# Attention scores from two rounded products of relu(m) and a linear part gathered with each source's row

## The reference, cut to what matters

```python
xl = (x @ Wl).reshape(n, H, D)
xr = (x @ Wr).reshape(n, H, D)
msg = xl[src] + xr[dst]
act = jnp.where(msg > 0, msg, NEG_SLOPE * msg)
e = jnp.einsum('ehd,hd->eh', act, att)
m = jax.ops.segment_max(e, dst, num_segments=n)
p = jnp.exp(e - m[dst])
denom = jax.ops.segment_sum(p, dst, num_segments=n)
alpha = p / (denom[dst] + 1e-16)
out = jax.ops.segment_sum(alpha[..., None] * xl[src], dst, num_segments=n)
```

## Time and profile before

| | |
|---|---|
| median of 3 runs | 1490.02 (1489.29 to 1491.17) |
| the profiled execution, its own time | 1491.28 |
| its span in the trace | 1489.5 |
| TensorE (PE) busy, share of the span | 1410.9, 95% |
| VectorE (DVE) | 781.9, 52% |
| ScalarE (ACT) | 424.5, 29% |
| GpSimd (POOL) | 255.5, 17% |
| the chain that ended last | PE 57%, DVE 1%; its lines L1946 35%, L1967 18% are the dense layers |

### The profile page before, as it was taken

The page is one execution under the profiler, slowest core; times in us unless marked ns, Lnnn a source line. Parts: engine busy times, 40 slices in busy tenths (PEclk is TensorE's granted clock), DMA queues, the critical chain, the costliest instruction groups (busy, mean ns, idle before and its releaser), DMA issues.

```text
span 1489.5 us, 17808 instructions
## 1 busy us (share of the span) xinstructions
PE 1410.9 (95%) x6845; PEld 1144.6 (77%) x6845; DVE 781.9 (52%) x1359; ACT 424.5 (29%) x716; POOL 255.5 (17%) x307
## 2 busy tenths in 40 slices
PE   3888999959999999899999999999999999999997
PEld 3886888836666666678888888888888888888886
DVE  6996777538888888645346621410133332410244
ACT  7862323246666664212111100201200000210000
POOL 3000000057777673100000000000010100000000
PEclk9997999979999999999999999999999999999999
DMA  1666344456556652432127443230066544400253
GB/s 48 188 181 207 107 106 140 96 161 212 167 167 172 208 170 70 144 121 95 54 92 248 157 182 116 90 114 0 1 217 221 183 130 142 159 1 0 78 191 128
DMA packets 102404, 195.97 MB, mean 132 GB/s; under 512 B 27143, under 2 KB 61752, under 8 KB 102320
## 3 DMA queue, kind: packets, MB, share of 16 engines
q1 hardware_dynamic: 77866, 121.28, 27.2%
q0 software_dynamic: 22640, 73.09, 14.2%
q10 hardware_dynamic: 1814, 0.47, 0.2%
HBM read 140.87 MB, written 53.92 MB: 131 GB/s over the span
## 4 chain that ended last, share of the span: by engine, by line
PE 57%; DVE 1%; DMA 0%; DVEq 0%; issue 0%; ACT 0%; POOL 0%
PE layers_y_ps L1946 35%; PE layers_y_ps L1967 18%; PE layers_turn_ps L1930 2%; PE layers_up_ps L1913 1%; PE layers_y_ps L1983 1%; DMA x_d<-fetched_x 0%; DVE layers_w_lo L2102 0%; DVE layers_y L2146 0%; PE layers_y_ps L1991 0%; DVE layers_y L605 0%; DVE layers_ln_stats L599 0%; PE layers_turn_ps L1901 0%; DVE layers_parts_lo L2119 0%; DVEq L600 0%; PE layers_y_ps L1901 0%
## 5 line engine op out<-in xcount | busy, mean ns | idle before, releaser
L517 POOL DMA_INDIRECT attention_got<-xl_d,heads_first_src x156 | 162.1, 1039 | 61.6 <-issue 43.8
L1967 PE MATMUL layers_y_ps<-layers_parts_hi,layers_counts 128*128 128x512 f32 x464 | 143.0, 389 | 0.0
L1967 PE MATMUL layers_y_ps<-layers_parts_lo,layers_counts 128*128 128x512 f32 x464 | 142.9, 389 | 0.0
L1946 PE MATMUL layers_y_ps<-layers_w_hi,layers_parts_hi 128*128 128x512 f32 x400 | 125.4, 395 | 0.0
L1946 PE MATMUL layers_y_ps<-layers_w_lo,layers_parts_hi 128*128 128x512 f32 x400 | 123.3, 389 | 0.0
L1946 PE MATMUL layers_y_ps<-layers_w_hi,layers_parts_lo 128*128 128x512 f32 x400 | 123.2, 389 | 0.0
L1967 PEld LDWEIGHTS layers_y_ps<-layers_parts_lo,layers_counts 128*128 128x128 f32 x464 | 87.1, 188 | 18.1
L1967 PEld LDWEIGHTS layers_y_ps<-layers_parts_hi,layers_counts 128*128 128x128 f32 x464 | 86.9, 188 | 17.9
L2119 DVE SCALAR_TENSOR_TENSOR layers_parts_lo<-layers_y_ps,layers_parts_hi 128x1024 fp32r<-128x1024 f32 x16 | 19.6, 1225 | 144.7 <-ACT layers_parts_hi L2062 144.7
L1334 PE MATMUL attention_row_ps<-attention_bent,edges_att_rows 128*128 128x512 f32 x184 | 95.4, 601 | 0.0
L1367 PE MATMUL attention_mix_ps<-attention_weighted,attention_hot 128*110 128x260 f32 x368 | 95.1, 382 | 0.0
(11 more groups left out here) (338 smaller groups left out, 2792.1 us busy)
## 6 DMA issues: line engine op xcount, KB each, us to landing
layers_counts<-counts_d SPq DMA_DIRECT2D x30, 640.0 KB, 4.0
layers_rest<-x_d SPq DMA_DIRECT2D x23, 512.0 KB, 3.9
self_d<-layers_y POOLq DMA_DIRECT2D x20, 512.0 KB, 5.6
x_d<-layers_y POOLq DMA_DIRECT2D x19, 512.0 KB, 2.9
fetched_x<-x_d SPq DMA_DIRECT2D x17, 512.0 KB, 3.6
fetched_raw<-in_L_gnn_W_self POOLq DMA_DIRECT2D x16, 512.0 KB, 5.7
fetched_raw<-in_L_gnn_W_neigh POOLq DMA_DIRECT2D x16, 512.0 KB, 8.9
heads_dst_wide<-in_dst_held SPq DMA_DIRECT2D x13, 512.0 KB, 4.6
```

The lines of the kernel that those rows point to most:

```text
L517: nc.gpsimd.indirect_dma_start(got[:, t, :], None, xl_d, bass.IndirectOffsetOnAxis(src[:, a * QUAD + t:a * QUAD + t + 1], 0))\
L1946: last = nc.tensor.matmul(y_ps[n % 2][:, a:a + HALF], rows_in[t][:, k * P:(k + 1) * P], w[k][:, a:a + HALF], start=(k == 0 and p == 0), st ...
L1967: last = nc.tensor.matmul(y_ps[n % 2][:, a:a + HALF], counts[c % 2][:, k, :], part[k][:, a:a + HALF], start=(k == 0 and part is hi), stop= ...
```

## The change

It uses act = 0.2 m + 0.8 relu(m). The linear part 0.2 m . att is 0.2 xl . att of the source plus 0.2 xr . att of the target. The target's is the same for all edges of a target and leaves the softmax as it is, so it is left out. The source's is computed once per node in the front, stored in 16 more columns of the node's row in xl_d (of which 4 are used, a row is now 1088 B) and so gathered with it; ScalarE copies it out of `got` (`take_linear`, twice a visit) and TensorE turns it as the first part of `row_ps` (`turn_linear`). For relu(m), ScalarE makes the rounded part (`bent_hi`) and VectorE the remainder (`bent_lo`), and the score is two f32r products in place of one float32 product. The attention vector is split in a rounded and a low part as well, placed in two sets of rows; `pick` sums the two sets in `spread`, and a 128x8 matrix `fold` sums them in `turn`, which is now a float32 product with 8 moving columns and no longer a transpose. The diff, cut to its core:

```diff
+XL_ROW = HID + LINE
...
+            nc.vector.tensor_scalar(g["folded_row"][:, :], row[:, :], float(QUADS * HEADS), -float(QUADS * HEADS),
+                                    ALU.is_ge, ALU.mult)
             dve.drain()
+            nc.vector.tensor_tensor(g["folded_row"][:, :], g["folded_row"][:, :], row[:, :], ALU.add)
...
             nc.vector.tensor_scalar(g["pick"][:, :, :],
                                     g["iota"][:, 0:QUADS * HEADS].unsqueeze(2).to_broadcast([P, QUADS * HEADS, PART]),
-                                    row[:, :], None, ALU.is_equal)
+                                    g["folded_row"][:, :], None, ALU.is_equal)
+            nc.vector.tensor_scalar(g["fold"][:, :], g["iota"][:, 0:QUADS * HEADS], g["folded_row"][:, :], None,
+                                    ALU.is_equal)
...
-        xl = m.sb("xl", [P, 2, HID])
+        xl = m.sb("xl", [P, 2, XL_ROW])
...
             def store_heads(tile):
                 u = tile % 2
-                sp.wait_ge(s["xl_ready"], tile + 1)
+                sp.wait_ge(s["linear_ready"], tile + 1)
                 sp.dma_start(rows(xl_d, tile), xl[:, u, :]).then_inc(xl_stored[u], 16)
...
                 dve.wait_ge(s["xl_ready"], tile + 1)
-                nc.vector.tensor_tensor(loop_sum[:, :], xr_ps[:, :], xl[:, u, :], ALU.add)\
+                linear = xl[:, u, HID:HID + HEADS]
+                nc.vector.scalar_tensor_tensor(out=linear_sum, in0=xl[:, u, 0:HID], scalar=SLOPE,
+                                               in1=att_row[:, :], op0=ALU.mult, op1=ALU.mult)
+                nc.vector.tensor_tensor(loop_sum[:, :], xr_ps[:, :], xl[:, u, 0:HID], ALU.add)\
                     .then_inc(s["xr_ready"], 1)
                 dve.drain()
-                nc.vector.scalar_tensor_tensor(out=loop_sum[:, :], in0=loop_sum[:, :], scalar=SLOPE,
-                                               in1=loop_sum[:, :], op0=ALU.mult, op1=ALU.max)
+                nc.vector.tensor_reduce(linear, linear_sum.rearrange("p (h d) -> p h d", h=HEADS), AX.X, ALU.add)\
+                    .then_inc(s["linear_ready"], 1)
+                nc.vector.tensor_scalar(loop_sum[:, :], loop_sum[:, :], 0.0, 1.0 - SLOPE, ALU.max, ALU.mult)
                 dve.drain()
...
-                                        AX.X, ALU.add).then_inc(s["xr_whole"], 1)
+                                        AX.X, ALU.add)
+                dve.drain()
+                scores = loop_score[:, u, :].rearrange("p (t k) -> p k t", t=2)
+                nc.vector.tensor_tensor(scores, scores, linear.rearrange("p (k t) -> p k t", t=2), ALU.add)\
+                    .then_inc(s["xr_whole"], 1)
...
-                    nc.vector.tensor_copy(g["att_rows"][r:r + PART, k, HEADS + h:HEADS + h + 1], att[r:r + PART, k:k + 1])
+                    nc.vector.tensor_scalar(g["att_rows"][r:r + PART, k, HEADS + h:HEADS + h + 1],
+                                            att[r:r + PART, k:k + 1], 1.0 - SLOPE, None, ALU.mult)
+                dve.drain()
+                for h in range(HEADS):
+                    k, r = h // 2, h % 2 * PART
+                    nc.vector.scalar_tensor_tensor(
+                        out=g["att_rows"][r:r + PART, k, 3 * HEADS + h:3 * HEADS + h + 1], in0=att[r:r + PART, k:k + 1],
+                        scalar=1.0 - SLOPE, in1=g["att_rows"][r:r + PART, k, HEADS + h:HEADS + h + 1].bitcast(F32),
+                        op0=ALU.mult, op1=ALU.subtract)
...
-        got = [first_got] + slots("got", [P, QUAD, HID], F32, GOT - 1)
+        got = [first_got] + slots("got", [P, QUAD, XL_ROW], F32, GOT - 1)
...
-        nothing = m.sb("nothing", [ROWS - SUB * SUBS, HEAD_DIM])
+        nothing = linear[0:ROWS - SUB * SUBS, 0, P - HEAD_DIM:]
...
+        def shifted_rows(j):
+            return far[j % 3][:, 0:HALF]
...
+            def turn_linear(j):
+                pe.wait_ge(linear_ready, QUADS * (j + 1))
+                for t in range(QUAD):
+                    nc.tensor.matmul(row_ps[j % 2][:, t * P:(t + 1) * P], linear[:, t, :], g["ident"][:, :],
+                                     is_transpose=True, start=(t == 0), stop=False, skip_group_check=True)
+
             def score(i):
                 j, a, k = i // UNITS, i % UNITS // KH, i % KH
                 pe.wait_ge(bent_ready, i + 1)
-                nc.tensor.matmul(row_ps[j % 2][:, :], g["att_rows"][:, k, (1 - a) * HEADS:(1 - a) * HEADS + P],
-                                 bent[i % 3][:, :], start=(i % UNITS == 0), stop=(i % UNITS == UNITS - 1),
-                                 skip_group_check=True).then_inc(scored, 1)
+                for part in (bent_hi, bent_lo):
+                    last = nc.tensor.matmul(row_ps[j % 2][:, :], g["att_rows"][:, k, (1 - a) * HEADS:(1 - a) * HEADS + P],
+                                            part[i % len(part)][:, :], start=False,
+                                            stop=(i % UNITS == UNITS - 1 and part is bent_lo), skip_group_check=True)
+                last.then_inc(scored, 1)
...
-                    last = nc.tensor.matmul(row_ps[j % 2][:, t * P:(t + 1) * P], shifted_rows[:, t * P:(t + 1) * P],
-                                            g["ident"][:, :], is_transpose=True, start=(t == 0),
+                    last = nc.tensor.matmul(row_ps[j % 2][:, t * P:t * P + QUADS * HEADS],
+                                            shifted_rows(j)[:, t * P:(t + 1) * P], g["fold"][:, :], start=(t == 0),
                                             stop=(t == QUAD - 1), skip_group_check=True)
...
+                if q == 2 and i < LAST:
+                    turn_linear(j)
                 if 2 <= i < LAST + 2:
                     score(i - 2)
...
-                nc.scalar.activation(scaled[i % 2][:, :], message_ps[i % 2][:, :], ACT.Copy, scale=SLOPE)\
-                    .then_inc(scaled_ready, 1)
+                nc.scalar.activation(bent_hi[i % 3][:, :], message_ps[i % 2][:, :], ACT.Relu).then_inc(high_ready, 1)
+
+            def take_linear(j, a):
+                act.wait_ge(*gathered(j, a))
+                nc.scalar.activation(linear[:, :, a * HEADS:(a + 1) * HEADS], held(j, a)[:, :, HID:HID + HEADS],
+                                     ACT.Copy).then_inc(linear_ready, 1)
...
                 if i < LAST:
                     scale(i)
+                if q == 0 and i < LAST:
+                    if j == 0:
+                        act.wait_ge(linear_cleared, 1)
+                    take_linear(j, 0)
...
                 if q == 1 and 1 <= j <= SUBS:
                     take_rows(j - 1)
+                if q == 1 and i < LAST:
+                    take_linear(j, 1)
...
             def bend(i):
-                dve.wait_ge(scaled_ready, i + 1)
-                nc.vector.tensor_tensor(bent[i % 3][:, :], message_ps[i % 2][:, :], scaled[i % 2][:, :], ALU.max)\
+                dve.wait_ge(high_ready, i + 1)
+                if i >= 2:
+                    dve.wait_ge(scored, i - 1)
+                nc.vector.scalar_tensor_tensor(out=bent_lo[i % 2][:, :], in0=message_ps[i % 2][:, :], scalar=0.0,
+                                               in1=bent_hi[i % 3][:, :].bitcast(F32), op0=ALU.max, op1=ALU.subtract)\
                     .then_inc(bent_ready, 1)
...
-                                        held(j, half)[:, :, :].rearrange("p t (h d) -> p (t h) d", h=HEADS),
+                                        held(j, half)[:, :, 0:HID].rearrange("p t (h d) -> p t h d", h=HEADS),
...
-            nc.vector.memset(nothing[:, :], 0.0).then_inc(nothing_made, 1)
+            nc.vector.memset(linear[:, :, :], 0.0).then_inc(linear_cleared, 1)
...
-    xl_d, mixed_d = dram("xl_d", [ROWS, HID]), dram("mixed_d", [ROWS, HID])
+    xl_d, mixed_d = dram("xl_d", [ROWS, XL_ROW]), dram("mixed_d", [ROWS, HID])
```

More of the change, by code:

```diff
@@ L636, in front_stage @@
         loop_sum = m.sb("loop_sum", [P, HID])
+        linear_sum = w.raw[:, KB - 1, :]
         loop_score = m.sb("loop_score", [P, 2, HEADS])
@@ L909, in take_heads @@
                     act.wait_ge(xl_stored[u], 16 * (tile // 2))
-                nc.scalar.activation(xl[:, u, :], xl_ps, ACT.Copy).then_inc(s["xl_ready"], 1)
+                nc.scalar.activation(xl[:, u, 0:HID], xl_ps, ACT.Copy).then_inc(s["xl_ready"], 1)
             split_x(0)
@@ L1066, in limit_edges @@
                 nc.vector.tensor_copy(g["rounds"][:, 1:2], rounds[:, :])
+            nc.vector.memset(xl[:, :, HID:], 0.0)
             split_x(0)
@@ L1266, in _ @@
             load(2)
[L1267 removed]
+            sp.wait_ge(linear_cleared, 1)
             for h in range(HEADS):
[L1269 removed]
+                sp.dma_start(mixed_d[SUB * SUBS:ROWS, h * HEAD_DIM:(h + 1) * HEAD_DIM], nothing)\
                     .then_inc(nothing_stored, 16)
@@ L1459, in take_shifted @@
                 act.wait_ge(shifted, j + 1)
-                nc.scalar.activation(shifted_rows[:, :], row_ps[j % 2][:, :], ACT.Copy).then_inc(shifted_out, 1)
```

(1 more changed line is left out.)

39 lines of the change are left out of this document (19 added, 20 removed).

## The result

The changed kernel took 1497.38 (median of 7 runs, 1494.16 to 1499.55) beside 1489.29 of the kernel before (7 runs, 1488.87 to 1491.17): ratio 1.0049, interval 1.0037 to 1.006. Its profiled execution took 1497.38 with a span of 1495.6, 6.1 above the span of before. It is slower by 8, inside the range, by more than the +1.4 of the sum.

What follows compares the result with a forecast made beforehand. DVE's chain, not PE, was taken to pace attention's visits. Terms 0.15 + 2.75 - 0.5 - 2.8 + 0.8 + 1.0 = +1.4 gave a median of 1491.4; range 1488.5 to 1498.8.

Steps and rivals of the forecast that it cites:

- the 0.67: Attention: DVE's wait per visit for the spread product, a DVE-PE-DVE round trip that stays; 13.4 to 14 in 20 visits.
- the -2.8 for arrears: Attention, visits 3 to 22: shorter scores save only the 2.8 us that a PE queue in arrears cost DVE.
- The clamp's slip: Attention: the longer turn delays the clamp by 0.08 in the ten visits without a weight half on DVE, +0.8 together.
- more than two: Attention, a sign of the forecast: DVE waits for the turn in more than two visits.
- 2 x 0.33: Attention: the turn's +0.33 shows whole in two visits where DVE already waited and in the tail, 3 x 0.33 = +1.0.
- The start's -0.5: Visits 0 and 1 of attention: a good quarter of PE's saving, twice 0.9, shows; -0.5 (0 to -1.8).
- I had taken 0.11: Turn: eight f32 weight loads at 0.11 each (0.108 as taken), making the turn 0.93 against 0.60.
- The Trainium skill's other rule that I weighed: POOL's gathers: 1088 B rows off 256 B boundaries need 16% more fetching, 1.04 would become 1.21 a gather.
- +2.75: Front's end and hand-over: +1.4 from DVE's longer steps and 1.35 from the xl store's wait; bounds 2.4 to 3.2.
- The first part: Hand-over: DVE's added work delays dt_lo(8), for which PE waits, by +0.85 (0.77 to 0.94).
- In the middle tiles it lies in DVE's waits for PE: Front, middle tiles: DVE's added +0.85 per tile is hidden in its waits for PE and costs nothing.
- The slower rival: Attention: the turn sets the clamp, loads at 188 ns each, clamp slips 0.65 in ten visits; 1498.8, chance 0.16.

Runs made afterwards that it cites:

- before_again: The kernel before, run once more unchanged for a second profile: 1488.92 in its one execution.
- turn_as_transpose: The changed kernel with the turn as four transposes again, as in the kernel before, the fold of the two row sets left out: 1492.07 in one execution.
- no_linear_in_front: The changed kernel without the source's linear part in the front, xl stored once copied: 1492.55, ratio 1.0015.
- after_shifted64: The changed kernel with one unused 64 B tile per partition, so later tiles of front and attention start 64 B higher: 1497.05, ratio 1.0046.
- front_at_old_addresses: The changed kernel with 192 unused bytes ahead of the front's tiles, putting them at the addresses of the kernel before: 1495.15, ratio 1.0039.
- spread_first_changed: The changed kernel with the first two spread products issued ahead of unit 2's messages on TensorE: 1492.19, ratio 1.0013.

## Why the prediction was right or wrong

**Right in its mechanism: attention.** DVE's chain is the pace, and the 0.67 is a round trip. Against the -2.8 for arrears the waits fell by 2.6, to 13.6 where 13.4 to 14 was named; a second cut of PE's work changed nothing. The clamp's slip was put at +0.08 a visit and measured +0.11; clamps waited for the turn in three visits, as "more than two" said, the first two and the last, and the waits of the first two grew by 0.6 for 2 x 0.33. The start's -0.5 isn't shown: att to c2, where it and those two clamps fall, is unchanged (48.47 for 48.51 in before_again). From c2 to c22 my terms make -1.7 (-2.8, +0.8 and one 0.33), and it came out at -0.4: without the f32 turn (turn_as_transpose) the stretch is 2.2 shorter than before, for the 2.8, and the turn takes 1.7 of that back, for the 1.1. Gathers (1019 ns for 1039), bend (683) and weigh cost nothing more.

The turn's eight loads stand in 1.08, the last 0.19 of it, so 0.13 from one to the next; I had taken 0.11. Weight loader, the transposing turn of turn_as_transpose:

```profile
467.57 0.58 PEld L1393 LDWEIGHTS attention_row_ps<-all_ident,attention_far 128*128 128x128 f32 x4
```

Four loads ahead of products of 128 moving columns stand in 0.58, the last 0.14 of it: 0.15 from one to the next. The Trainium skill ("TensorE: Matmul & The Clock Gate", "LDWEIGHTS (loading the stationary operand)") says that a load's time follows the stationary columns alone. The trace agrees in so far as 8 moving columns in place of 128 left the loads about as far apart, 0.13 for 0.15. The Trainium skill's other rule that I weighed ("DMA: Bandwidth & Descriptors", "How a descriptor splits into AXI transactions"), by which rows that start off a 256 B boundary are dearer to fetch, doesn't show in the gather's time on POOL, nor in the median from issue to landing, 3.4 in both kernels.

**Right: the hand-over.** +2.75 was forecast. It is +2.6 in the profiled pair (20.58 to 23.18), and again between before_again and turn_as_transpose (19.27 to 21.88). The first part was put at 0.85 and measured 0.77 (2.94 - 2.17), the low end of its range.

**Wrong: the front.** The step that failed is "In the middle tiles it lies in DVE's waits for PE". It costs 0.9 there (no_linear_in_front): in a tile in which DVE was already late the longer `take_heads` stands ahead of `scale_down`, and PE waits 0.84 for it. I had looked at DVE's waits on average and not at the tile with the least of them. Beside it the sum lacks a term: products that the change doesn't touch were costed at nothing, and some 1.6 came from where the front's tiles lie.

**Missing: the clock.** In more of the profiles with the change than without, TensorE's clock fell at the hand-over, behind the longer wait for `dt_lo`, and early in attention (last section). Stage by stage the change costs 2.5 + 0.2 + 2.6 - 0.6 + 0.2 = 4.9 (both profiles have the fall at the hand-over). The result gave 8.1, after_shifted64 6.6. The mean granted clock of each execution points to the clock for the rest: in the later executions of the kernel before, 27 at 0.981 took 1491.3 on average and 17 at 0.984 took 1488.7, and the seven of the changed kernel are all at 0.977 to 0.979. By that slope the 0.004 between the medians of the two kernels (0.978 and 0.982) would be some 3 of the 8. This is an estimate from executions that may differ in other ways as well; no run shows it.

The slower rival's number, 1498.8, lies near the result, and its mechanism isn't there: no turn delays the clamp by 0.65, and loads stood 0.13 apart, not 0.188. That the range held is luck: its upper end came from that rival.

## What to carry to other kernels

Before a saving is booked, find the wait that ends the stage's visit: here it was a round trip between two engines, and a change of order worth four lines gained more than the new arithmetic. Work that is put "into the waits" of a repeated stage must be checked against the iteration with the least slack, not the mean one. After a change, compare rows that the change doesn't touch as well: a tile more or less ahead of them moves their operands.

## What the runs showed of the hardware that was not expected

**Where tiles lie in SBUF changed the pace of products.** In the middle tiles of the front the 16 f32r products of `w_lo`, 512 columns each, took 3.79 to 3.80 with the front's tiles, the stationary `xt` among them, where the kernel before has them (seven profiles). With these tiles 192 or 128 bytes lower or 64 higher they took 3.87 to 3.90 (seven profiles), 2 to 3% more. The moving operands `w_hi` and `w_lo` lie at the other end of SBUF and weren't moved. Four placements don't settle which rule this is, and how it acts wasn't tried.

**After the same idle time the clock fell in some executions and not in others.** Windows view at the products after PE's wait for `dt_lo`, changed kernel (wait 1.96); columns as in the earlier trace rows, the granted clock third from the end:

```profile
298.40:300.40 2.00, 2.00 (x12) 2.00 (x11) 0.30 (x1) 0.00 (x0) 0.00 (x0) 0.50 0.25 70
```

The kernel of turn_as_transpose, the same wait of 1.96:

```profile
297.00:299.00 2.00, 2.00 (x20) 2.00 (x19) 0.94 (x2) 0.64 (x2) 0.00 (x0) 1.00 0.45 136
```

0.50 is the lower of the clock's two levels, 1.2 GHz, 1.00 the upper, 2.4. Behind the wait of 1.96 the clock fell in 5 of 6 profiles (in front_at_old_addresses only 1.5 after the products had begun); behind 1.27 in the one profile of no_linear_in_front; behind 1.19, before's, in 1 of 4; behind 0.26 in none of 3. These are too few to tell the effect of the wait's length from chance. One fall costs 1.3 from y9 to g (20.58 for 19.27 in two profiles of the same kernel; 23.18 for 21.88 in the changed kernel and turn_as_transpose, whose fronts are the same). The second place is early in attention, spread_first_changed and the changed kernel:

```profile
345.00:348.00 3.00, 3.00 (x10) 2.41 (x10) 2.51 (x3) 1.45 (x5) 2.54 (x2) 0.50 0.93 260
```

```profile
347.26:350.26 3.00, 3.00 (x20) 2.49 (x19) 2.32 (x7) 2.47 (x2) 2.28 (x3) 1.00 0.50 151
```

Ten products ran in 3 us at the lower level, twenty (not the same ones) at the upper. The clock fell near there in 6 of 9 profiles with the change and in none of 5 without, and these six took 48.1 to 51.4 from att to c2, the others 48.0 to 49.4. Why it fell more often with the change is open.
